# One convolution block and an expert layer on one core: constant matmuls in TensorE's waits, the centring matrix first, rounding and token numbers of the router shared with ACT, output stores issued by ACT

## The reference

```python
x = x + conv_ref(ln_c(x))            # ln_c: layer norm over the 64 channels of each pixel
t = tokens(x)                        # 16384 tokens of 64 channels
t = t + ffn_ref(ln_t(t))
# conv_ref(x): two rounds of
#   quant_act(batchnorm(.)): clip to 0..1, round to 15 levels; batch mean and variance over all pixels
#   conv3x3 with weights tanh'd, scaled by their maximum, rounded to 15 levels, masked with a pattern
#   and + x at the end
# ffn_ref(x): router logits (8 experts), softmax, top 2, gates renormalised;
#   y_e = w2_e @ (silu(w1_e @ x) * (w3_e @ x)) with 682 hidden units; sum of the two gated results
```

## Time and profile before

| | us |
|---|---|
| median of three runs (lowest, highest) | 844.22 (844.14, 847.58) |
| the profiled execution | 845.35 |
| its span, first to last instruction | 843.3 |
| TensorE busy | 754.9 (90%) |
| VectorE busy | 568.3 (67%) |
| GpSimd busy | 541.0 (64%) |
| ScalarE busy | 483.7 (57%) |
| mean granted TensorE clock | 0.925 |

### The profile page before, as it was taken

How to read it: one execution, slowest core, us unless ns; L and a number is a source line. 1 busy time by engine, 2 the same in 40 slices (tenths; PEclk the granted TensorE clock), 3 DMA queues, 4 the chain that set the end, 5 groups by cost and what they waited for, 6 DMA issues and landing times.

```text
span 843.3 us, 17635 instructions
## 1 busy us (share of the span) xinstructions
PE 754.9 (90%) x4875; PEld 438.7 (52%) x4875; DVE 568.3 (67%) x1494; ACT 483.7 (57%) x1042; POOL 541.0 (64%) x564
## 2 busy tenths in 40 slices
PE   5959678988199999999999999999999999999924
PEld 3744266666044554545454554545454547777623
DVE  4976578888556666666666666667676666666535
ACT  5736447565156666666666666666666566666500
POOL 3530017777777777777777777777777777777510
PEclk9959889887589999999999999999999999999955
DMA  8660013333244434333343444333433346656269
GB/s 199 129 117 0 0 60 98 118 105 113 90 127 122 131 112 125 114 114 114 113 116 110 124 113 119 112 116 114 113 114 110 115 131 179 192 170 186 74 240 357
DMA packets 84226, 105.54 MB, mean 125 GB/s; under 512 B 27061, under 2 KB 57966, under 8 KB 84176
## 3 DMA queue, kind: packets, MB, share of 16 engines
q1 hardware_dynamic: 65040, 83.47, 34.2%
q0 software_dynamic: 19136, 21.54, 9.1%
HBM read 73.90 MB, written 27.30 MB: 120 GB/s over the span
## 4 chain that ended last, share of the span: by engine, by line
PE 75%; DVE 12%; issue 5%; DMA 2%; ACT 2%; SPq 2%; POOL 1%; DVEq 1%; POOLq 0%; ACTq 0%
PE bank L1384 40%; PE bank L1399 21%; PE bank L1270 5%; PE bank L1365 3%; PE bank L1357 2%; PE bank L1210 2%; DMA conv_all<-result_rows 1%; SPq L481 1%; PE bank L1215 1%; DVE stats L976 1%; PE bank L1226 1%; PE bank L1284 1%; DVE y_and_rows L963 1%; DMA w<-expert_w 0%; DVE stats L820 0%
## 5 line engine op out<-in xcount | busy, mean ns | idle before, releaser
L546 POOL DMA_INDIRECT expert_rows<-y_and_rows,slot_all x256 | 249.8, 976 | 145.4 <-issue 77.1
L1133 DVE TENSOR_TENSOR conv_all<-conv_all,bank 128x512 f32<-128x512 f32 x340 | 233.4, 687 | 153.0 <-ACT conv_all L713 151.8
L1384 PE MATMUL bank<-xT,w 64*128 64x512 f32 (+1 forms) x1608 | 327.4, 537 | 1.9 <-DMA w<-expert_w 1.7
L713 ACT ACTIVATE conv_all<-bank 128x512 f32<-128x512 f32 x340 | 203.1, 597 | 119.3 <-PE bank L1384 118.7
L1384 PEld LDWEIGHTS bank<-xT,w 64*128 64x128 f32 x1608 | 145.3, 187 | 172.9 <-DVE conv_all L1133 84.8
L556 POOL DMA_INDIRECT result_rows<-conv_all,dest_all x142 | 140.0, 986 | 50.9 <-issue 41.5
L1399 PE MATMUL bank<-conv_all,w 128*64 128x256 f32 x1240 | 161.7, 384 | 1.2 <-DVE tile_map L1102 1.2
L1399 PEld LDWEIGHTS bank<-conv_all,w 128*64 128x64 f32 x1240 | 91.1, 136 | 51.7 <-issue 12.6
L724 ACT ACTIVATE xT<-bank 64x256 f32<-64x256 f32 x272 | 103.0, 379 | 18.9 <-PE bank L1357 16.5
L1270 PE MATMUL bank<-quant_padded,conv_w_blocks 128*128 128x512 bf16 x288 | 69.2, 399 | 8.7 <-issue 4.4
L556 POOL DMA_INDIRECT result_rows<-squares,dest_all x64 | 63.1, 986 | 20.3 <-issue 19.4
(11 more groups left out here) (245 smaller groups left out, 855.5 us busy)
## 6 DMA issues: line engine op xcount, KB each, us to landing
w<-expert_w SPq DMA_DIRECT2D x68, 384.0 KB
w<-expert_w SPq DMA_DIRECT2D x68, 192.0 KB
conv_all<-expert_rows SPq DMA_DIRECT2D x56, 136.0 KB
x_all<-in_x SPq DMA_DIRECT2D x16, 256.0 KB, 4.1
x_all<-y_and_rows POOLq DMA_DIRECT2D x16, 256.0 KB, 4.3
expert_rows<-y_and_rows,slot_all POOLq DMA_INDIRECT x256
y_and_rows<-result_rows SPq DMA_DIRECT2D x8, 512.0 KB, 9.6
conv_all<-result_rows SPq DMA_DIRECT2D x8, 512.0 KB, 10.5
```

The source lines that it names most:

```text
L546: nc.gpsimd.indirect_dma_start(xs, bass.IndirectOffsetOnAxis(ap=slot_all[:, s, k * GH + g:k * GH + g + 1], axis=0), rows_all[:, s, g, :], ...
L713: nc.scalar.activation(sbuf[k % 3], h1_ps[k % 3][:], ACT.Silu).then_inc(silu_rdy, 1)
L1133: V.tensor_tensor(hbuf[k], sbuf[k % 3], h3_ps[k % 3][:], ALU.mult).then_inc(mul_rdy, 1)
L1384: ins = mm(ps[k % 3][:, rows_], w[half, cols], xT[u][half, rows_], start=True, stop=True)
```

## The change

SP loads the convolution weights right behind the first pair of x, on a semaphore of their own, for which ACT's tanh waits. POOL announces the identity as soon as it is made, DVE makes `centre` first of its constants, and PE's first centring waits for `centre` alone; the other constants are awaited ahead of the first `var`. Some steps of the first pairs are reordered on PE and ACT, and the root's table is loaded ahead of the first root. `keep_busy(n, bank)` issues n matmuls of 512 columns in bf16 on constant data, whose results nobody reads: 10 ahead of each `pair_up` and 18 behind it, 30 ahead of the first `turn_map` and 16 behind it, 10 behind the turn of the first tile's rows; 10 matmuls of 128 columns in f32 with the identity stand at the start. `batch_norm` has fewer one-column steps. In the router loop the padding moves from DVE to ACT (`pads`, between the exponentials and the squares; DVE keeps the rounding), as do writing and adding the token numbers (`tokens`, `exps`). The output stores move from SP to ACT's queue.

```diff
+                if p == 0:
+                    for k, w in enumerate((w1, w2)):
+                        sp.dma_start(wc[:, k, :], w.rearrange("o i a b -> o (i a b)")).then_inc(wc_in, 16)
                 if p == 1:
-                    for k, w in enumerate((w1, w2)):
-                        sp.dma_start(wc[:, k, :], w.rearrange("o i a b -> o (i a b)")).then_inc(small_in, 16)
                     sp.dma_start(pati[:], pat.rearrange("a b -> (a b)").partition_broadcast(C)).then_inc(small_in, 16)
...
-            for p in range(NP):
-                sp.wait_ge(o_rdy, 2 * p + 6)
-                for h in range(2):
-                    sp.dma_start(outv[h, p], xb[64 * h:64 * h + 64, 2 * S * p:2 * S * (p + 1)]
-                                 .rearrange("c (i p) -> c i p", i=2 * IMG)).then_inc(o_out, 16)
             sp.wait_ge(o_out, 32 * NP)
...
+            pool.sem_inc(ident_rdy, 1)
...
-            act.wait_ge(small_in, 16 * NSMALL)
+            act.wait_ge(wc_in, 32)
...
-            square(0)
-            square(1)
+            square(0, 0)
+            square(0, 1)
+            act.wait_ge(centre_rdy, 1)
+            load_table(ACT.Sqrt)
+            keep_centred(0, 0)
+            sd(0)
+            keep_centred(0, 1)
+            centred(1)
             for p in range(NP):
-                sd(p)
+                if p:
+                    sd(p)
                 if p + 2 < NP:
-                    square(p + 2)
+                    centred(p + 2)
...
+            def pads(p):
+                for u in range(2):
+                    s = 2 * p + u
+                    act.wait_ge(round_rdy, s + NS + 1)
+                    act.wait_ge(cv_rdy, s + NS + 1)
+                    nc.scalar.activation(qpad[u][:, :, 1:H + 1, 1:W + 1],
+                                         qt[u][:].rearrange("p (i a b) -> p i a b", i=IMG, a=H),
+                                         ACT.Copy, bias=-ROUND).then_inc(qp_rdy, 1)
+
+            def tokens(p):
+                nc.scalar.activation(of_pair(rows_all, p)[:, :, C], token[:], ACT.Copy)
+
             def exps(p):
                 act.wait_ge(ex_go, p + 1)
                 nc.scalar.activation(lg[:], lg[:], ACT.Exp)
-                nc.scalar.activation(top2[:], top2[:], ACT.Exp).then_inc(ex_rdy, 1)
+                nc.scalar.activation(ratio[:], top2[:], ACT.Exp).then_inc(ex_rdy, 1)
+                nc.scalar.activation(token[:], token[:], ACT.Copy, bias=float(4 * S))
...
+                tokens(p)
                 if first:
                     exps(p)
                 if last != 1:
...
+                if not last:
+                    pads(p + 2)
                 if last != 1:
...
+            for p in range(NP):
+                act.wait_ge(o_rdy, 2 * p + 6)
+                for h in range(2):
+                    nc.scalar.dma_start(outv[h, p], xb[64 * h:64 * h + 64, 2 * S * p:2 * S * (p + 1)]
+                                 .rearrange("c (i p) -> c i p", i=2 * IMG)).then_inc(o_out, 16)
...
+            V.memset(same_half[:], 0.0)
+            one(V.memset(half_col[:], 0.0))
+            V.memset(half_col[0:64, 0:1], 1.0 / C)
+            V.memset(half_col[64:128, 1:2], 1.0 / C)
+            V.memset(same_half[0:64, 0:64], 1.0 / C)
+            one(V.memset(same_half[64:128, 64:128], 1.0 / C))
+            dve.wait_ge(ident_rdy, 1)
+            V.tensor_tensor(centre[:], ident[:], same_half[:], ALU.subtract).then_inc(centre_rdy, 1)
...
-                one(V.bn_aggr(mv[:, l, :], bn[:, l].rearrange("p s n -> p (s n)")))
-                V.tensor_copy(mv2[:, l, 0:1], mv[:, l, 0:1])
-                V.scalar_tensor_tensor(mv2[:, l, 1:2], mv[:, l, 0:1], mv[:, l, 0:1], mv[:, l, 1:2],
+                one(V.bn_aggr(mv2[:, l, :], bn[:, l].rearrange("p s n -> p (s n)")))
+                V.scalar_tensor_tensor(mv2[:, l, 1:2], mv2[:, l, 0:1], mv2[:, l, 0:1], mv2[:, l, 1:2],
                                        ALU.mult, ALU.add).then_inc(agg_rdy, 1)
                 dve.wait_ge(pr_rdy, l + 1)
-                t = bt[:, l, :]
-                mean, m2_ = mv[:, l, 0:1], mv[:, l, 1:2]
+                mean, square = mv[:, l, 0:1], mv[:, l, 1:2]
+                var_, sd_, r, w, minus_mean, beta_, scaled_r = (bt[:, l, k:k + 1] for k in range(7))
                 one(V.tensor_copy(mv[:, l, :], bank[6][:, 0:2]))
-                one(V.tensor_tensor(t[:, 0:1], mean, mean, ALU.mult))
-                one(V.tensor_tensor(t[:, 0:1], m2_, t[:, 0:1], ALU.subtract))
-                V.tensor_scalar(t[:, 0:1], t[:, 0:1], of * of, 1e-5, ALU.mult, ALU.add).then_inc(bva_rdy, 1)
+                one(V.scalar_tensor_tensor(var_, mean, mean, square, ALU.mult, ALU.subtract))
+                V.tensor_scalar(var_, var_, -of * of, 1e-5, ALU.mult, ALU.add).then_inc(bva_rdy, 1)
+                V.tensor_scalar(minus_mean, mean, -1.0, None, ALU.mult)
+                V.tensor_scalar(beta_, gb[:, 2 * l + 1:2 * l + 2], LEVELS, None, ALU.mult)
                 dve.wait_ge(bsd_rdy, l + 1)
-                one(V.reciprocal(t[:, 2:3], t[:, 1:2]))
-                one(V.scalar_tensor_tensor(t[:, 3:4], t[:, 0:1], -0.5, t[:, 2:3], ALU.mult, ALU.mult))
-                one(V.tensor_tensor(t[:, 3:4], t[:, 3:4], t[:, 2:3], ALU.mult))
-                one(V.scalar_tensor_tensor(t[:, 2:3], t[:, 3:4], 1.5, t[:, 2:3], ALU.add, ALU.mult))
-                one(V.tensor_scalar(t[:, 2:3], t[:, 2:3], gb[:, 2 * l:2 * l + 1], LEVELS * of, ALU.mult, ALU.mult))
-                V.tensor_copy(aff[:, l, 0:1], t[:, 2:3])
-                one(V.tensor_tensor(t[:, 3:4], mean, t[:, 2:3], ALU.mult))
-                V.scalar_tensor_tensor(aff[:, l, 1:2], gb[:, 2 * l + 1:2 * l + 2], LEVELS, t[:, 3:4],
-                                       ALU.mult, ALU.subtract).then_inc(aff_rdy, 1)
-
-            q_chain = chain("vector_quant")
+                one(V.reciprocal(r, sd_))
+                V.tensor_scalar(scaled_r, r, gb[:, 2 * l:2 * l + 1], LEVELS * of, ALU.mult, ALU.mult)
+                one(V.scalar_tensor_tensor(w, var_, -0.5, r, ALU.mult, ALU.mult))
+                one(V.tensor_tensor(w, w, r, ALU.mult))
+                one(V.scalar_tensor_tensor(aff[:, l, 0:1], w, 1.5, scaled_r, ALU.add, ALU.mult))
+                V.scalar_tensor_tensor(aff[:, l, 1:2], minus_mean, aff[:, l, 0:1], beta_,
+                                       ALU.mult, ALU.add).then_inc(aff_rdy, 1)
+
+            q_chain = Chain()
+            q_chain.sem = round_rdy
...
-                quant = [lambda f=f, u=u: f(1, 2 * p + 4 + u, u) if not last else None
-                         for f in (quant_round, quant_pad) for u in range(2)]
+                quant = [lambda u=u: quant_round(1, 2 * p + 4 + u, u) if not last else None for u in range(2)]
...
-                  lambda: V.tensor_copy(rows_p[:, :, C], token[:]))
+                  )
...
-                  lambda: V.tensor_scalar(token[:], token[:], float(4 * S), None, ALU.add).then_inc(ex_go, 1))
+                  lambda: dve.sem_inc(ex_go, 1))
...
-                else:
-                    quant[2]()
-                    quant[3]()
...
-            pe.wait_ge(const_p, 1)
-            pe.wait_ge(const_v, 1)
-
+            def keep_busy(n, ps):
+                for _ in range(n):
+                    mm(ps[:], ident_bf[:], wblk[:, 0, 0:4, :].rearrange("p t c -> p (t c)"), start=True, stop=True)
+
+            pe.wait_ge(ident_rdy, 1)
+            for _ in range(10):
+                mm(bank[4][:, 0:128], ident[:], ident[:], start=True, stop=True)
+            pe.wait_ge(centre_rdy, 1)
...
+            pe.wait_ge(const_p, 1)
+            pe.wait_ge(const_v, 1)
+            var(0)
             pe.wait_ge(wm_rdy, 1)
             mm(wmt_ps, wmax[:], ident[0:C, 0:C], start=True, stop=True).then_inc(wmt_rdy, 1)
...
+                if p == 0:
+                    spread(0)
                 if p + 1 < NP:
                     var(p + 1)
-                spread(p)
+                if p:
+                    spread(p)
...
+            keep_busy(10, bank[2])
             pair_up(0)
+            keep_busy(18, bank[2])
             pipelined(pe, lambda s, u: conv(0, s, u), lambda s, u: None, NS)
+            keep_busy(10, bank[2])
             pair_up(1)
+            keep_busy(18, bank[2])
...
+            keep_busy(30, bank[0])
             turn_map(0, bank[5][0:1, 0:128], bank[5][:, 128:256])
+            keep_busy(16, bank[0])
...
             turn(0, 0).then_inc(xt_rdy, 1)
+            keep_busy(10, bank[0])
             tiles(pe, tile)
```

52 lines of the change are left out of this document (26 added, 26 removed).

## The result

The changed kernel takes 839.87 us, median of five runs (838.94 to 840.04); the kernel before, run beside it on the same chip, takes 845.47. The ratio is 0.9926, 95% interval 0.9904 to 0.9948: about 0.7% faster, 5.6 us. The forecast was 834.4 with a range of 829.5 to 840.5, so the result lies 0.6 us inside the slow end of the range. The profiled execution is 840.04 us with a span of 838.0, so between the two profiles 5.3 us are gained where the sum expected 9.8.

A forecast was written before the change was run, and what follows sets the result against it. Tiles are TensorE-bound and untouched, so gains come only from seams, router loop and tail. Terms 3.3 + 0.3 + 2.2 + 3.5 + 0.4 + 2.6 - 2.5 = 9.8 off 845.35 gave 835.5, or 834.4 on the median; range 829.5 to 840.5.

The forecast's parts named there:

- Part 1: Start: first centring waits only for the centring matrix and first x stripes, variances 4.0 us earlier; 3.3 us gained.
- Part 2: First batch norm and convolution: convolution starts 2.05 us late behind constant matmuls but gains 2.35 running warm; net 0.3 gained.
- Part 3: Second batch norm: ten constant matmuls covered, eighteen take 4.0 us, two convolutions 4.0 instead of 5.64; 2.2 us gained.
- Part 4: Router loop: VectorE gives up paddings in passes 1 to 5, and ACT's squares stay in time; 3.5 us gained.
- Part 5: Map and first tile: map's turning nets 0.4 us, and the first tile's 24 matmuls run faster, 2.6 net.
- The rival of the clock lost in that gap: Before the first tile: the clock falls again, the ten constant matmuls run cold and only delay; 837.0 us, chance 0.16.
- Part 6: GpSimd beside the tiles: its queue shifts 5.8 us, the tiles 12.3; with 7.6 us of slack it just follows.
- Part 7: Tail: ACT's stores share DMA engines with loads, period 4.06 us, last load late and its chain uncovered; 2.5 us lost.
- The clock's rule: First batch norm: transposes do not count as work for the clock as matmuls do, so it falls without a TensorE gap.

The follow-up runs named there:

- start held: Changed kernel with the maxima turned ahead of the first variance matmuls and three constant 512-column matmuls in the wait behind them: 840.72 us, ratio 0.9933.
- every gap held: Changed kernel with stores on SP, constant matmuls added at start, first stage's end, router passes and map, fewer at first batch norm: 831.26 us, ratio 0.9817.
- router held: Changed kernel with ten constant 256-column matmuls ahead of the positions in router passes 1 to 7: 838.72 us, ratio 0.9899.

## Why the prediction was right or wrong

The direction was right and the time lies in the range, close to its slow end; of the gain of 9.8 us in the sum, 5.3 came. The mechanisms were those put down, but the sum took it for granted that nothing else becomes late, and the granted clock made it so in three stretches (start, first batch norm, router loop). That it comes out no worse is in part luck: the clock and the loads of the tail make single executions of one stretch differ by as much as the misses.

**Part 1, start (3.3 forecast, 1.0 measured).** The order of events was as put down: centring at 6.12, x's second pair the next wait (0.53 us), the variances 3.4 us earlier where the part took 4.0, VectorE's steps on the maxima waited for (0.52). Missing is what those short waits and two-column matmuls do to the clock: the profile shows it at 1.00 up to 42 us before, and it fell from 14 to 18 us after. Two groups of matmuls pay 1.7 us for it. The experiment with the start held gives 2.1 as the value with the clock up, so 1.1 of the miss is the clock and the other 1.2 is size: 0.6 at the variances, and the rest behind them, where TensorE now waits 1.0 us for VectorE at the end of stage 1 (ahead of 43.82 in that kernel) and worked through before.

**Part 2, first batch norm and convolution (0.3, -0.7).** The ten cold and their queue effect were right (pairing at 57.30, 4.44 behind the rows, forecast about 4.6). The eighteen were taken wholly at the full clock and took 4.65 instead of 4.0. The convolution was expected to gain 2.35 and gained 1.6: its 144 matmuls take 32.55 us, 0.226 each, not 31.8. The term for the later start (2.05) measured 2.3. The shorter chain, put at 0.64, gives 0.45 in the run without constant work. The ten are the loss: leaving them out gives 0.3 to 1.6 us.

**Part 3, second batch norm (2.2, 1.9).** Right in each step: ten covered, eighteen in 4.04, convolutions in 4.2 for two instead of 5.64. The run without constant work gives all but 0.1 of it back.

**Part 4, router loop (3.5, 2.3).** The paddings' worth is right, 0.6 to 1.0 us a pass in the run with them on VectorE, and so is that ACT keeps up. The step that failed is the silent one that nothing else becomes late. The low stretches of the clock met the turning of rows before, and now meet two convolutions (6.85 and 5.63 us instead of 4.21). That the shorter passes shift them there is what the profiles suggest, not what they show, since one with the longer passes has it too. The one makes its pass 1.3 us longer than its neighbours (14.10 against 12.77), the other about 0.9 (12.19 against the 11.3 with every gap held; 11.70 in the kernel before).

**Part 5, map and first tile (0.4 + 2.6 forecast, 2.5 measured).** Right, and all of it constant work. The ten behind the turn of the first rows ran warm and the first tile's first twelve matmuls took 2.85 us. The rival of the clock lost in that gap (0.16) did not come in this profile but did in the one with the router held.

**Part 6, GpSimd.** Right: its shift is 2.1 us against 6.9 of the tiles, its waits fell from 9.1 to 5.0, 4.1 where the difference is 4.8, and it did not end last.

**Part 7, tail (-2.5, -1.7).** Two sizes failed, in opposite senses, and that the total came near is luck. The period was expected at 4.06 us five times and is 3.9 three times and 3.05 once: 3.9 us in all instead of 6.75, to which the first period, without a store on the way, adds 0.8. The chain behind the last load was taken at 4.1 us to the last addition and 3.3 to land, 7.4 together, and takes 8.8 (829.20 to 838.0). Both terms are right (829.20 to 833.17, and 3.2 from 834.78 to 838.0); missing between them is the issue of the last two stores, 1.6 us, which ACT can begin only when the addition is done. The idle DMA engines in this gap were foreseen, and the slices above show them. The Trainium skill (DMA: Bandwidth & Descriptors, Queues, rings and completion order) has each DMA engine take turns between queues and take each queue in order; the stretched period with two queues and the even 2.70 us with one agree with that.

**The clock's rule.** The Trainium skill (TensorE: Matmul & The Clock Gate, Part 4: PE-mode transpose) does not count transposes as work for the clock the way it counts matmuls. The kernel before agrees: its clock falls at about 43.8 us, within two-column matmuls and transposes that follow each other without a gap from 40.5 to 48.5 us (0.92 in the window from 42 to 44, 0.50 in the next). The changed kernel doesn't show it as clearly, since TensorE waits there for 0.98 and 1.63 us in the same stretch. In the run with every gap held wide matmuls stand both between these transposes and in these waits, and its window from 0 to 50.6 us is at 1.00; that run doesn't tell the transposes from the waits.

What stays open: why the clock falls at 14.5 us in some executions and not in others with the same instructions, and stays low for 6.8 us (116.9 to 123.7, changed kernel) or for 13.6 (stores on SP) at the beginning of the router loop. Where it falls goes a long way to explain why executions of one kernel differ: 840.35 to 848.31 us in ten runs without constant work (mean granted clock 0.933 in the fastest, 0.922 in the slowest), but 831.13 to 831.96 in five with every gap held. What sets the moment was not tried, nor why one pair of the tail's loads is late in some executions.

## What to carry over

In these runs constant matmuls paid where TensorE came warm into a wait that is longer than they are, and where a wide piece of work followed (second batch norm, map and first tile); queued cold ahead of a matmul that others wait for, they delayed it (first batch norm, 0.3 to 1.6 us). When gaps are filled, fill all of them: in the runs with one of them filled some later stretch was cold all the same, and with all of them filled five executions lay within 0.8 us. Leave stores that are due at the end on the queue of the loads ahead of them, so that they are issued before they can move and take nothing from the loads.
